# Self-attention stage: the first scores unit of step n+2 is issued on TensorE before the weightings of rounds 1 and 2 of step n

## The reference: one decoder layer

```
q, k, v = (xn @ W.T + b) split into 16 heads of 16
attn = q k^T * scale + rel          # rel: a 32 x 32 table per head, interpolated to 512 x 512
attn = softmax(where(j > i, -inf, attn))
out  = (attn @ v) @ Wo.T + bo
```

## Time and profile before

| what | value |
|---|---|
| three runs, median | 2689.03 us |
| the profiled execution, its own time | 2688.25 us |
| span of the profiled execution | 2686.3 us |
| PE busy over the span | 2568.6 us (96%) |
| PEld busy over the span | 2311.8 us (86%) |
| DVE busy over the span | 1937.6 us (72%) |
| ACT busy over the span | 1609.3 us (60%) |
| first score matmul of self-attention | 100.62 us |
| last `store` of self-attention | 333.01 us |

### The profile page before, as it was taken

One profiled execution on the slowest core, in us unless ns is written; L12 is line 12 of the kernel. 1 busy time (PEld: TensorE's weight loads), 2 busy tenths in 40 slices (PEclk: granted clock), 3 DMA queues, 4 the chain that ended last, 5 costly groups with the idle time before them and its releaser, 6 DMA issues. The chain is left out here.

```text
span 2686.3 us, 47091 instructions
## 1 busy us (share of the span) xinstructions
PE 2568.6 (96%) x17664; PEld 2311.8 (86%) x17664; DVE 1937.6 (72%) x3665; ACT 1609.3 (60%) x3056; POOL 123.2 (5%) x155
## 2 busy tenths in 40 slices
PE   6799979999999999999999999999999999999976
PEld 4699967998899889988999899988998899889975
DVE  6688877776777677777777677767776777677766
ACT  4599845556565656664656556646565665566646
POOL 0354010000000000000000000000000000000003
PEclk8899989999999999999999999999999999999997
DMA  4996342001200110002000300030002000110000
GB/s 160 249 193 148 78 170 92 17 16 64 71 17 16 61 66 24 16 32 95 17 19 14 118 17 16 16 110 24 16 16 104 31 16 16 75 47 24 8 13 32
DMA packets 89486, 156.72 MB, mean 58 GB/s; under 512 B 42721, under 2 KB 56289, under 8 KB 87777
## 3 DMA queue, kind: packets, MB, share of 16 engines
q1 hardware_dynamic: 84736, 141.26, 17.5%
q0 software_dynamic: 3248, 12.72, 1.4%
q10 hardware_dynamic: 1328, 0.39, 0.1%
HBM read 122.76 MB, written 27.39 MB: 56 GB/s over the span
## 5 line engine op out<-in xcount | busy, mean ns | idle before, releaser
L1347 ACT CAST pt_hi<-xt_ps 128x512 fp32r<-128x512 f32 x1024 | 592.5, 585 | 574.9 <-PE xt_ps L1317 558.9
L1413 DVE TENSOR_TENSOR pt_lo<-xt_ps,pt_hi 128x512 fp32r<-128x512 f32 x1024 | 704.8, 688 | 265.5 <-ACT pt_hi L1347 262.1
L1402 DVE TENSOR_SCALAR_CACHE_REDUCE xprobs<-xs_ps 128x1024 f32<-128x1024 f32 x512 | 626.7, 1224 | 175.0 <-PE xs_ps L1266 170.2
L1328 PE MATMUL xo_ps<-pt_hi,v_hi 128*128 128x256 f32 x2048 | 649.5, 317 | 1.3 <-DVE pt_lo L1413 1.3
L1353 ACT ACTIVATE xprobs<-xprobs,xneg_max 128x1024 f32<-128x1024 f32 x512 | 591.5, 1155 | 26.7 <-DVE xneg_max L1408 26.7
L1317 PE MATMUL xt_ps<-ident,xprobs 128*128 128x128 f32 x4096 | 604.2, 272 | 0.0
L1328 PE MATMUL xo_ps<-pt_lo,v_hi 128*128 128x256 f32 x2048 | 577.6, 282 | 0.0
L1328 PE MATMUL xo_ps<-pt_hi,v_lo 128*128 128x256 f32 x2048 | 576.0, 281 | 0.0
L1317 PEld LDWEIGHTS xt_ps<-ident,xprobs 128*128 128x128 f32 x4096 | 485.1, 140 | 60.7 <-issue 6.9
L1328 PEld LDWEIGHTS xo_ps<-pt_hi,v_hi 128*128 128x128 f32 x2048 | 388.8, 190 | 4.0 <-DVE pt_lo L1413 1.3
L1328 PEld LDWEIGHTS xo_ps<-pt_lo,v_hi 128*128 128x128 f32 x2048 | 389.4, 190 | 1.9
(11 more groups left out here) (201 smaller groups left out, 2659.1 us busy)
## 6 DMA issues: line engine op xcount, KB each, us to landing
v_split<-ctx_split SPq DMA_DIRECT2D x68, 768.0 KB, 5.7
xq<-x_split SPq DMA_DIRECT2D x64, 512.0 KB, 3.2
q_st<-rel_split SPq DMA_DIRECT2D x32, 256.0 KB, 4.0
q_st<-q_split SPq DMA_DIRECT2D x32, 192.0 KB, 4.5
k_st<-k_split SPq DMA_DIRECT2D x32, 192.0 KB, 4.9
ctx_split<-ctx_out POOLq DMA_DIRECT2D x8, 768.0 KB, 4.5
q_split<-stage_hi SPq DMA_DIRECT2D x4, 1024.0 KB, 9.2
k_split<-stage_hi SPq DMA_DIRECT2D x4, 1024.0 KB, 10.6
```

The lines of the kernel that those rows point to most:

```text
L1328: last = pe.matmul(o_ps[:, 0:GQ], v[:, vs], pt[:, c % 3, GQ * j:GQ * (j + 1)], start=c == 0 and j == 0 and m == 0, stop=c == PIECES - 1 an ...
L1347: act.copy(pt_hi[:, c % 3, :], t_ps[:, c % 3, :]).then_inc(t_rounded, 1)
L1402: dve.tensor_scalar(probs[:, par if kind == "A" else 1 - par, t, CHUNK * i:CHUNK * (i + 1)], s_ps[:, buf, :], LOGIT, None, ALU.mult, ALU.m ...
L1413: dve.tensor_tensor(pt_lo[:, c % 3, :], t_ps[:, c % 3, :], pt_hi[:, c % 3, :].bitcast(F32), ALU.subtract).then_inc(t_ready, 1)
```

## The change: one line of PE's order

`scores(n + 2, 0)` moves from behind `weigh(n, 2)` to before `weigh(n, 1)`. The orders of ACT, DVE, POOL and SP stay as they are.

```diff
@@ -589,9 +589,9 @@
             pe.wait_ge(keys_loaded, 16)
             for n in range(-2, STEPS):
                 turn(n, 4)
+                scores(n + 2, 0)
                 weigh(n, 1)
                 weigh(n, 2)
-                scores(n + 2, 0)
                 turn(n + 1, 0)
                 turn(n + 1, 1)
                 scores(n + 2, 1)
```

## The result

The changed kernel is slower: median 2703.78 us of 6 runs (2701.68 to 2704.29) against 2689.70 us of 6 runs of the kernel before. The ratio is 1.0053, with a 95% interval of 1.0040 to 1.0065. The medians are 14.1 us apart. The forecast was 14.3 us more, and a time of 2703 us. The profiled execution has a span of 2702.5 us against 2686.3.

A forecast was written before the change was run, and what follows sets the result against it. The bound was a 7.02 us ring of PE's and ACT's legs, joined by waits for exponentials and the last weighting. 29 x 0.50 + 0.34 - 0.52 = 14.3 us more gave 2703 us; range 2696 to 2711.

The forecast's parts named there:

- The moved wait comes back in every step: At L547 PE idles 0.66 us for unit 1 of the exponentials every step, both ends hanging on weigh(n, 4).
- Length of the ring: From unit 1's exponentials through moved scores, PE's work and store back to unit 1: a step takes 7.52 instead of 7.02 us.
- The first step: In the first affected step PE waits less for unit 1; the turns start at 116.03 instead of 115.69: +0.34 us.
- The old stall goes: One step with late values before weigh(., 0) took 7.54 us; the new wait swallows that stall: -0.52 us.
- PE does not let ready work pass: At L547 a semaphore wait holds back weightings behind it; the rival, ready work passing, kept 2689 us, 5 in 100.
- PE as its own bound: Rival: ACT comes ahead, the moved wait costs nothing and PE works without a gap; 2683.5 us, 3 in 100.
- earlier maxima: Rival: DVE's earlier maxima of unit 0 partly shorten ACT's way, giving back half the wait; 2696 us, 5 in 100.
- the clock: Rival: granted clock falls because PE idles 0.66 us of 7.52, doubling PE's leg of 4.9 us; 2836 us, 1 in 100.
- ACT's leg: ACT's unbroken work from store to the end of unit 1 of the exponentials, 2.55 us, without a wait for DVE.
- The sum of 14.3 us: Over the self-attention stage: 29 x 0.50 + 0.34 - 0.52 = 14.3 us slower, everything after only shifted.

The follow-up runs named there:

- five places on PE: unit 0 scores before turn(n, 4), as changed, between the weightings, as before, behind turn(n+1, 0): steps 7.94, 7.56, 7.10, 7.02, 7.84 us.
- unit 1 earlier on ACT: Changed kernel, with ACT making unit 1 of the exponentials before rounding round 2, and DVE the maxima of unit 2 before round 2's rest: 2693.05 us.
- the control to it: Kernel before with its own PE order, plus ACT making unit 1 before round 2 and DVE maxima of unit 2 before round 2's rest: 2717.47 us.
- late values: SP loads values of step n+1 only when scores(n+2, 1) is done: 2733.56 us on the kernel before, 2745.19 us on the changed one.
- the scores one place earlier: Changed kernel with the scores of unit 0 also moved before turn(n, 4): 2715.84 us, ratio 1.0103.

## Why the prediction was right, point by point

*The moved wait comes back in every step.* Right. Forecast were an idle of 0.66 us and a wait "some 29 times"; the trace has 0.65 us on the weight loads, 28 times in the stretch. The five places on PE, together with unit 1 earlier on ACT and the control to it, show the cause: the price follows what stands behind the wait and when unit 1 ends, not the order as such.

*Length of the ring.* 7.56 us against 7.52. The sum over-counted one gain: the eight transposes without a wait take 0.82 us (321.73 to 322.55), not 0.79. Four score matmuls after a wait take 0.74 (319.94 to 320.68) instead of 0.72, the six weightings 1.05 instead of 1.07. The remaining hundredths lie in terms that differ by 0.01 or 0.02 us, which is the rounding of the rows. Over 29 steps the rings grew by 14.97 + 0.52 = 15.5 us, since the kernel before had one stalled step among them; forecast were 14.5.

*The first step.* The term is right. Unit 1 ends at 114.28 + 1.57 = 115.85, and the turns start 1.82 us later, at 117.67:

```profile
115.89 0.50 PE L547 MATMUL s_ps<-k_st,q_st 112*128 112x512 f32 x1 [0.34 <-ACT probs L619]
...
117.67 0.52 PE L563 MATMUL t_ps<-ident,probs 128*128 128x128 f32 x3
```

Forecast were 1.84 us (116.03 - 114.19), and before it was 1.50. The first `store` is 2.01 us later all the same: 0.82 by the later start, 0.84 by the clock that rose later, 0.35 by the move. The forecast had no term for the first two.

*The old stall goes.* The size is right: all distances between `store` rows of the changed kernel up to step 29 are 7.54 to 7.56 us, and the 7.54 us outlier of the earlier trace rows among 7.02 has no counterpart. The mechanism is shown for the stalls of the late values. In the profiled execution of the changed kernel the values were not late at all, so there was nothing to swallow, and that the -0.52 us came true in it is luck. In two other traces stalls came by themselves in front of a short wait for unit 1, and were not swallowed: a step of 7.57 us among 7.09 with the scores between the weightings, and steps of 7.76 and 7.82 among 7.11 with unit 1 earlier on ACT.

*PE does not let ready work pass.* Right: the weightings start at 320.68, behind the scores. *PE as its own bound*, *earlier maxima* and *the clock* did not occur: ACT's leg kept its 2.53 us, and the clock stayed at 1.00 from 127.6 us to the end of the stage.

The sum of 14.3 us meets the 14.1 us between the medians partly by luck. In the traces the stage from the first score to the last `store` grew by 248.54 - 232.39 = 16.15 us, where about 14 were forecast: 1.0 us is the ring that came out longer, 0.84 the clock that rose later. The rest of the kernel gives +0.8 ahead of the stage and -0.8 behind it. The spans differ by 16.2 us, and the profiled execution of the changed kernel is the slowest of its six (2704.29).

## What to carry to other kernels

Where engines work through fixed orders in a ring, ask of each wait what ready work stands behind it. If a waiting instruction is moved ahead of such work, the ring through its wait grows by the length of that work, and the step grows as soon as this ring is the longest: 7.02, 7.10, 7.56 and 7.94 us with none, one and two weightings and then the transposes behind the wait. Read both ends of the wait back to the event that they start from; if it is the same one, the wait comes back every round. And when a piece is taken out of a ring, look at what the waiting engine waits for next: the wait of `store` only moved to round 2. PE's busy time before, 198.13 of 199.22 us, told none of this; five places for the same four matmuls gave steps from 7.02 to 7.94 us.

## What was not expected of the hardware

With late values in the kernel before, waits of PE's weight loads of up to 4.2 us appeared in the first half of the stage, and there the granted clock fell. The kernel before with late values, 120 to 200 us in stretches of 20 (columns as in the earlier trace rows):

```profile
120.00:140.00 20.00, 16.14 (x111) 14.65 (x110) 13.94 (x21) 15.41 (x35) 12.20 (x14) 0.94 0.71 154
140.00:160.00 20.00, 15.28 (x99) 14.08 (x98) 11.38 (x17) 11.53 (x25) 13.21 (x15) 0.89 0.47 115
160.00:180.00 20.00, 17.73 (x131) 16.35 (x131) 13.96 (x21) 15.56 (x34) 10.37 (x13) 1.00 0.73 206
180.00:200.00 20.00, 14.12 (x86) 12.86 (x86) 11.30 (x18) 12.20 (x28) 9.48 (x11) 0.81 0.72 175
```

The longest waits for values in these four stretches were 3.31, 4.20, 1.76 and 4.21 us. With waits of 0.65 to 1.29 us in every step, as in the changed kernel and in the one with the scores one place earlier, the clock had stayed at 1.00. It also stayed at 1.00 in each stretch of 20 us from 120 to 320 us of the changed kernel with late values, whose waits were 2.20 us at most. In the kernel before with late values a load of `v_st` took 3.3 us from issue to landing in the first half (median, 120 to 240 us; 5.6 at most) and 2.3 in the second (2.4 at most). POOL's transfers of 768 KB each ran only in the first half; that they held up the values is likely, but no run shows it.
